# A graph attention and convolution kernel: the second ffn layer as three f32r passes, one slot for the spread row, new step orders

## The reference

```python
def _gat_heads(x, adj, W, a):                      # H heads
    Wh = einsum('bnf,hfo->bhno', x, W)
    e = f1[:, :, :, None] + f2[:, :, None, :]       # f1 = Wh.a[:O], f2 = Wh.a[O:]
    e = where(adj > 0, leaky_relu(e), -1e9)
    return softmax(e) @ Wh

h   = relu(layernorm(x))
h1  = elu(_gat_heads(h, adj, W_heads, a_heads))     # 4 heads, joined to 1024 features
out = elu(_gat_heads(h1, adj, W_out, a_out))        # 1 head, 256 features
ffn = relu(out @ w1 + b1) @ w2 + b2
x   = x + layernorm(ffn + out) * gamma + beta
h   = relu(layernorm(x))
x   = x + deg * (h @ Wi.T + b) + adj @ (h @ Wj.T)
```

## Time and profile before

| | |
|---|---|
| median of 3 runs | 1364.8 us (1364.24 to 1365.14) |
| profiled execution | 1362.21 us |
| its span | 1360.4 us |
| PE busy | 1305.1 us, 96% |
| weight loads (PEld) busy | 1254.3 us, 92% |
| DVE busy | 1095.9 us, 81% |
| ACT busy | 1116.3 us, 82% |
| POOL busy | 371.1 us, 27% |
| mean granted TensorE clock | 0.991 |

### The profile page before, as it was taken

The page is one execution under the profiler, slowest core; times in us unless marked ns, Lnnn a source line. Parts: engine busy times, 40 slices in busy tenths (PEclk is TensorE's granted clock), DMA queues, the critical chain, the costliest instruction groups (busy, mean ns, idle before and its releaser), DMA issues.

```text
span 1360.4 us, 27728 instructions
## 1 busy us (share of the span) xinstructions
PE 1305.1 (96%) x10109; PEld 1254.3 (92%) x10109; DVE 1095.9 (81%) x2848; ACT 1116.3 (82%) x2152; POOL 371.1 (27%) x252
## 2 busy tenths in 40 slices
...
DMA packets 42206, 53.32 MB, mean 39 GB/s; under 512 B 2836, under 2 KB 30808, under 8 KB 42072
## 3 DMA queue, kind: packets, MB, share of 16 engines
...
...
## 4 chain that ended last, share of the span: by engine, by line
PE 79%; DVE 10%; ACT 6%; issue 4%; DMA 1%; POOL 1%; SPq 0%; ACTq 0%; DVEq 0%; POOLq 0%
PE ps L1101 59%; PE ps L1214 8%; PE ps L1316 4%; PE ps L1280 3%; DVE arg L986 2%; DVE prob_lo L957 1%; ACT arg L785 1%; PE ps L1253 1%; PE ps L1290 1%; ACT prob_hi L791 1%; DVE arg L1012 1%; DVE st L939 1%; PE ps L1176 1%; DVE elu L1023 1%; DVE whx_lo L957 1%
## 5 line engine op out<-in xcount | busy, mean ns | idle before, releaser
L658 POOL TENSOR_TENSOR hx_lo<-elu,hx_hi 128x512 fp32r<-128x512 f32 x128 | 166.6, 1304 | 661.6 <-ACT hx_hi L815 660.4
L1101 PE MATMUL ps<-prob_hi,whx_hi 128*128 128x256 f32 x1024 | 296.0, 289 | 2.8 <-DVE prob_lo L957 2.1
L1101 PE MATMUL ps<-prob_hi,whx_lo 128*128 128x256 f32 x1024 | 289.6, 283 | 0.0
L1101 PE MATMUL ps<-prob_lo,whx_hi 128*128 128x256 f32 x1024 | 289.5, 283 | 0.0
L785 ACT ACTIVATE arg<-arg,nmax 128x512 f32<-128x512 f32 x320 | 226.9, 712 | 3.9 <-DVE nmax L997 3.7
L957 DVE TENSOR_TENSOR prob_lo<-ps,prob_hi 128x1024 fp32r<-128x1024 f32 x160 | 195.1, 1220 | 32.4 <-ACT prob_hi L791 32.1
L781 ACT ACTIVATE arg<-arg,fcol 128x512 f32<-128x512 f32 x320 | 212.3, 714 | 8.5 <-DVE gmax L986 8.4
L986 DVE CUSTOM_DVE_ANT_0 arg<-f2bc,mask 128x512 f32<-128x512 f32 x308 | 207.3, 710 | 3.6 <-PE ps L1214 3.0
L1101 PEld LDWEIGHTS ps<-prob_hi,whx_hi 128*128 128x128 f32 x1024 | 195.9, 191 | 6.5 <-DVE prob_lo L957 3.8
L1101 PEld LDWEIGHTS ps<-prob_hi,whx_lo 128*128 128x128 f32 x1024 | 196.1, 191 | 0.3
L1101 PEld LDWEIGHTS ps<-prob_lo,whx_hi 128*128 128x128 f32 x1024 | 195.9, 191 | 0.0
...
## 6 DMA issues: line engine op xcount, KB each, us to landing
...
f_rows<-f2row SPq DMA_DIRECT2D x77, 2.0 KB
...
```

The lines of the kernel that those rows point to most:

```text
L658: pool.tensor_tensor(out=hx[1][:, 2 * c.h:2 * c.h + 2, c.u * HN:(c.u + 1) * HN], in0=elu[:, c.buf, :, :], in1=hx[0][:, 2 * c.h:2 * c.h + 2 ...
L1101: i = pe.matmul(out, a, b_, start=(k == 0), stop=(k == n - 1))
```

## The change

The second ffn layer uses `product` as well: `w2` is split once into `w2w` (high and low part), and `midT` is a pair of f32r tiles. To make them, ACT now writes the relu back to PSUM in place, waits for it, and copies it rounded to SBUF as the high part; DVE subtracts that from PSUM to get the low part. `midT` lies in the buffers of `outT`, which `ffn1` has finished reading by then. The PSUM pair of `ffn1` is released by the low part (`mid_lo`), not by the relu. `f2bc` has one slot in place of two. The place where w1 is staged moves to the one slot, and w2 is staged in a part of `arg`. All orders of steps (FIRST, ROUND, LAST) are new; ROUND_FROM, ROUNDS go from 8, 8 to 10, 7.

```diff
-    F2S = 2
+    F2S = 1
-        w2_sb = sb("w2_sb", [P, KC, F])
+        w2w = [sb(f"w2_{s}", [P, KC, F], f32r) for s in ("hi", "lo")]
-        w1_st = f2bc[:, 1, :].rearrange("p (k o) -> p k o", k=KC)
+        w1_st = f2bc[:, 0, :].rearrange("p (k o) -> p k o", k=KC)
+        w2_st = arg[:, 2, 1, :].rearrange("p (k o) -> p k o", k=KC)
-        midT = ff[:, 1, :, :].rearrange("p c f -> p (c f)").rearrange("p (k n) -> p k n", k=KC)
+        midT = outT
 ...
             def w1_prep(c):
                 act.wait_ge(ld[LD_W1], 16)
                 act.activation(w1x[0][:, :, :], w1_st, ACT.Copy).then_inc(s_w1_hi, 1)
+                act.wait_ge(ld[LD_W2], 16)
+                act.activation(w2w[0][:, :, :], w2_st, ACT.Copy).then_inc(s_w1_hi, 1)
 ...
                     act.wait_ge(f1_done, KC * (c.n - 1) + o + 1 if len(c.tiles) == NC else KC * c.n)
-                    act.activation(midT[:, o, c.cols], ffn1_out(c, o), ACT.Relu,
-                                   bias=b1c[:, o:o + 1]).then_inc(f1_read, 1)
+                    act.activation(ffn1_out(c, o), ffn1_out(c, o), ACT.Relu, bias=b1c[:, o:o + 1]).then_inc(f1_relu, 1)
+                for o in range(KC):
+                    act.wait_ge(f1_relu, KC * (c.n - 1) + o + 1)
+                    i = act.activation(midT[0][:, o, c.cols], ffn1_out(c, o), ACT.Copy)
+                i.then_inc(mid_hi, 1)
 ...
             def w1_low(c):
                 dve.wait_ge(s_w1_hi, 1)
                 dve.tensor_tensor(out=w1x[1][:, :, :], in0=w1_st, in1=w1x[0][:, :, :].bitcast(fp32), op=ALU.subtract).then_inc(s_w1, 1)
+                dve.wait_ge(s_w1_hi, 2)
+                dve.tensor_tensor(out=w2w[1][:, :, :], in0=w2_st, in1=w2w[0][:, :, :].bitcast(fp32), op=ALU.subtract).then_inc(s_w1, 1)
 ...
+            def ffn1(c):
+                dve.wait_ge(mid_hi, c.n)
+                for o in range(KC):
+                    i = lo(midT[1][:, o, c.cols], ffn1_out(c, o), midT[0][:, o, c.cols])
+                i.then_inc(mid_lo, 1)
 ...
-                lend((c.pair,), (f1_read, KC * c.n))
+                lend((c.pair,), (mid_lo, c.n))
 
             def ffn2(c):
                 if c.b == 0:
-                    pe.wait_ge(ld[LD_W2], 16)
-                pe.wait_ge(f1_read, KC * c.n)
+                    pe.wait_ge(s_w1, 2)
+                pe.wait_ge(mid_lo, c.n)
 ...
-                    for k in range(KC):
-                        i = pe.matmul(y, midT[:, k, n * P:(n + 1) * P], w2_sb[:, k, :], start=(k == 0), stop=(k == KC - 1))
+                    i = product(y, [(midT[0][:, k, n * P:(n + 1) * P], midT[1][:, k, n * P:(n + 1) * P], w2w[0][:, k, :], w2w[1][:, k, :])
+                                    for k in range(KC)])
```

The order of PE in the repeating period, before and after, begins differently but is the same round:

```diff
-    f2turn:2@5 turn_p:2@5 m1:00@4 turn_gc@7 turn_p:3@5 m1:01@4 attend:2@5 conv_in:0@7 f2turn:3@5 conv_in:1@7 turn_p:4@6
-    attend:3@5 m1:10@4 turn_p:5@6 attend:4@6 turn_p:6@5 f2turn:0@4 attend:5@6 m1:11@4 conv@7 turn_out@6 attend:6@5 turn_p:7@5
-    turn_p:8@5 ffn1@6 f2turn:1@4 attend:7@5 attend:8@5 turn_p:9@5 m1:20@4 m1:21@4 ffn2@6 m1:30@4 attend:9@5 mix2:0@5
-    turn_p:0@4 mix2:1@5 turn_p:1@4 mix2:2@5 mix2:3@5 attend:0@4 f2turn:-1@5 m1:31@4 turn_in@3 attend:1@4
+    f2turn:1@5 attend:7@6 attend:8@6 turn_p:9@6 ffn2@7 m1:20@5 m1:21@5 attend:9@6 mix2:0@6 m1:30@5 mix2:1@6 turn_p:0@5
+    mix2:2@6 turn_p:1@5 mix2:3@6 attend:0@5 m1:31@5 f2turn:-1@6 turn_in@4 attend:1@5 f2turn:2@5 turn_p:2@5 m1:00@4 turn_gc@7
+    turn_p:3@5 m1:01@4 attend:2@5 conv_in:0@7 turn_p:4@6 f2turn:3@5 conv_in:1@7 attend:3@5 turn_p:5@6 m1:10@4 attend:4@6
+    turn_p:6@5 attend:5@6 m1:11@4 f2turn:0@4 conv@7 turn_out@6 attend:6@5 turn_p:7@5 turn_p:8@5 ffn1@6
```

```diff
+    f2turn:0@5 args:8@6 turn_out@7 elu_neg:6@6 elu_exp:6@6 probs:7@6 args:9@6 probs:8@6 ffn1@7 f2turn:1@5 elu_neg:7@6
...
+    probs:2@7 m1:00@6 rowmax:4@8 turn_gc@9 rowmath:4@8 rowmax:5@8 probs:3@7 m1:01@6 rinv:4@8 scale:4@8 rowmath:5@8 elu_out:2@7
+    conv_in:0@9 rowmax:6@7 rinv:5@8 rowmath:6@7 scale:5@8 probs:4@8 rowmax:7@7 conv_in:1@9 rinv:6@7 scale:6@7 elu_out:3@7
+    probs:5@8 norm_in@5 m1:10@6 elu_out:4@8 rowmath:7@7 probs:6@7 rowmax:8@7 rinv:7@7 rowmath:8@7 elu_out:5@8 scale:7@7
+    m1:11@6 rowmax:9@7 rinv:8@7 scale:8@7 conv@9 rowmath:9@7 turn_out@8 norm_in_out@5 elu_out:6@7 probs:7@7 rinv:9@7 probs:8@7
+    scale:9@7 rowmax:0@6 ffn1@8 elu_out:7@7 elu_out:8@7 rowmath:0@6 probs:9@7 rowmax:1@6 m1:20@6 ffn2@8 norm_ff@8 rinv:0@6
...
+    norm_in_out:1@0 mask:1@0 turn_in@0 w1_low@0 gc_turn@0 turn_in:1@0 m1:00@0 mask_end:1@0 norm_in@1 wo_prep:0@0 wo_prep:1@0
+    m1:01@0 wo_prep:2@0 wo_prep:3@0 rowmax:0@0 rowmath:0@0 m1:10@0 norm_in_out@1 rowmax:1@0 wo_prep:4@0 m1:11@0 rinv:0@0
...
+    turn_p:7@-1 turn_p:8@-1 ffn1@-2 attend:7@-1 attend:8@-1 turn_p:9@-1 ffn2@-2 attend:9@-1 mix2:0@-1 mix2:1@-1 mix2:2@-1
+    mix2:3@-1 f2turn:-1@-1 f2pe:-1@-1 turn_gc@-2 conv_in:0@-2 turn_p:4@-1 conv_in:1@-2 turn_p:5@-1 attend:4@-1 attend:5@-1
+    conv@-2 turn_out@-1 turn_out:1@-1 ffn1@-1 ffn1:1@-1 ffn2@-1 ffn2:1@-1 turn_gc@-1 turn_gc:1@-1 conv_in:0@-1 conv_in:1@-1
...
+    norm_ff@-2 hx_lo:9@-1 gamma@-2 norm_gc@-2 bias@-2 add_b2@-1 norm_ff@-1 x_beta@-1 norm_ff:1@-1 gamma@-1 gamma:1@-1
```

More of the change, by code:

```diff
@@ L19 @@
[L19 to L23, removed]
@@ L57 @@
+    m1:11@3 conv@0 rowmath:9@2 rinv:8@2 turn_out@1 scale:8@2 elu_out:6@2 probs:7@2 probs:8@2 rinv:9@2 rowmax:0@3 ffn1@1
+    elu_out:7@2 scale:9@2 rowmath:0@3 elu_out:8@2 probs:9@2 rowmax:1@3 ffn2@1 norm_ff@1 m1:20@3 rinv:0@3 rowmath:1@3 scale:0@3
+    elu_out:9@2 rowmax:2@3
     """,
     "POOL": """
-    norm_in@0 norm_in:1@0 norm_in@1 hx_lo:0@0 hx_lo:1@0 hx_lo:2@0 hx_lo:3@0 x_beta@0 hx_lo:6@0 hx_lo:7@0 hx_lo:8@0 hx_lo:9@0
-    norm_in@2 hx_lo:0@1 hx_lo:1@1 hx_lo:2@1 hx_lo:3@1 norm_in@3 hx_lo:6@1 hx_lo:7@1 add_b2@0 hx_lo:8@1 norm_ff@0 hx_lo:9@1
@@ L84 @@
+    elu_exp:7@6 hx:6@6
     """,
     "DVE": """
[L86 to L89 removed]
@@ L234 @@
-    scale:4@-1 conv@-2 rinv:5@-1 scale:5@-1 probs:4@-1 probs:5@-1 elu_out:4@-1 turn_out@-1 elu_out:5@-1 turn_out:1@-1 ffn2@-1
-    norm_ff@-1 norm_ff_out@-1 ffn2:1@-1 norm_ff:1@-1 x2@-1 norm_ff_out:1@-1 norm_gc@-1 x2:1@-1 norm_gc_out@-1 norm_gc:1@-1
-    norm_gc_out:1@-1 turn_gc@-1 turn_gc:1@-1 conv_in:0@-1 conv_in:1@-1 conv@-1 conv:1@-1
+    rinv:1@-6 m1:21@-6 m1:30@-6 norm_ff_out@-8 scale:1@-6 rowmath:2@-6 mix2:0@-7 rowmax:3@-6 rowmath:3@-6 probs:0@-6 x2@-8
+    probs:1@-6 rinv:2@-6 mix2:1@-7 norm_gc@-8 elu_out:0@-6 scale:2@-6 m1:31@-6 norm_gc_out@-8 rinv:3@-6 turn_in@-5 scale:3@-6
@@ new lines @@
+    conv@-6 rowmath:9@-4 scale:7@-4 scale:8@-4 turn_out@-5 elu_out:6@-4 probs:7@-4 probs:8@-4 rowmax:0@-3 rinv:9@-4 scale:9@-4
+    ffn1@-5 elu_out:7@-4 rowmax:1@-3 probs:9@-4 rowmath:0@-3 elu_out:8@-4 m1:20@-3 norm_in_out@-2 ffn2@-5 norm_ff@-5
+    rowmax:2@-3 norm_ff_out@-5 rinv:0@-3 rowmath:1@-3 rowmath:2@-3 elu_out:9@-4 scale:0@-3 m1:21@-3 rinv:1@-3 rowmax:3@-3
+    scale:1@-3 rowmath:3@-3 mix2:0@-4 probs:0@-3 m1:30@-3 x2@-5 norm_gc@-5 mix2:1@-4 rinv:2@-3 probs:1@-3 elu_out:0@-3
+    norm_gc_out@-5 m1:31@-3 rinv:3@-3 scale:2@-3 turn_in@-2 scale:3@-3 elu_out:1@-3 probs:2@-3 m1:00@-2 rowmax:4@-4
```

403 lines of the change are left out of this document (207 added, 196 removed).

## The result

The changed kernel takes 1370.6 us (median of 7 runs, 1368.0 to 1372.9), the kernel before, measured beside it, 1364.2 us (7 runs). The ratio is 1.0051, with a 95% interval of 1.0041 to 1.0061: slower by half a per cent, where 9.1 us less were forecast. Its profiled execution took 1371.99 us, with a span of 1370.2.

The account below looks back on a forecast made before the run. PE's own stream was taken as the bound in the middle, DVE in the first 70 us. Terms -8.9 (PE), +1.0 (start), -1.2 (tail) sum to -9.1: 1353.1 us profiled, 1355.7 us median, range 1349 to 1362.

Parts of the forecast that it names:

- PE's stream: ffn2 on PE: 24 f32r matmuls replace the float32 block, 2.87 for 3.46 us; 0.59 us less a batch, 8.9 over 15.
- The rival with 0.108 us a pass: ffn2's passes run at the float32 pace: 0.87 us saved a batch, 13.1 in all, 1351.5 us; chance 0.05.
- ACT and DVE: Added copies and subtractions, +1.2 and +1.3 us a period: 69.6 and 68.4 of some 78.8 us busy, no new bound.
- The wait at turn_p:9: PE waiting for mid_lo after ffn1: none taken, range 0 to 0.5 us a period; as rival 1360 us, chance 0.13.
- The slot: One slot for f2's broadcast: 5.5 us of DVE work covers issue and landing (3.6, 4.7 at worst), so zero cost.
- The rival's shape: Single slot makes broadcasts late at each of 77 hand-overs; at 0.2 us each 1371 us; chance 0.06.
- The start: DVE bounds the first 70 us and runs 2 to 4 us later; loss of 1 us taken; dearer-start rival 5 us, chance 0.10.
- The tail: Work behind the last mix2: 3.1 us less, then 1.9 more for x_beta between the norms; net 1.2 less.

Follow-up runs that it names:

- e2_orders: The changed kernel's orders and one slot for the spread f2, with the float32 second layer of the kernel before: 1378.1 us, ratio 1.0106.
- e4_slot: The kernel before with one slot for the spread f2 in place of two, nothing else changed: 1385.9 us, ratio 1.0165.
- The splices: Changed kernel, each engine following the old order up to a seam, then the new: seam at 22 us 1374.8 us, at 123 us 1360.8, at 259 us 1357.5.
- s1: Changed kernel with norm_in of batch 1 and wo_prep:0 to 3 moved later in VectorE's order of the start: 1371.0 us, ratio 1.0062.
- s2: Changed kernel with the whole adjacency chain (loads, cast, turn, wo_prep) and norm_in of batch 1 put later in the start: 1375.5 us, ratio 1.0086.
- h6_start_259: Changed kernel with the old order on all engines up to steps started there before 259 us, w2 staged in xb: 1357.5 us, ratio 0.9957.

## Why the prediction was wrong, step by step

- **PE's stream: right, a little large.** 0.59 us a batch were forecast. The block takes 2.94 us and saves 0.52, the period 0.50, since the first matmul of the step needs 0.21 to the next and not 0.12. It does so behind the float32 transposes of `turn_p:9`; where another product stands ahead of it (976.12), the first needs 0.12 and the block takes 2.85. 15 times 0.50 are 7.5, and after against e2_orders measured 7.5. That the two agree to the digit is luck: the new orders with the float32 layer have a period of 79.34, so the passes alone save 0.44, and from a0 to the end the two profiles differ by 5.0. The rival with 0.108 us a pass is out: between 729.92 and 732.53 are 22 steps of 0.1186.
- **ACT and DVE: right, DVE 1.2 too high.** 69.53 and 67.25 busy in the period, 69.6 and 68.4 forecast.
- **The wait at turn_p:9: none, as taken.** PE is busy 78.90 of 78.90. The closeness of the working (0.1 us) was a warning all the same: in the old orders the passes with this chain cost 15.5 us.
- **The slot: nothing, as taken, and for the reason given.** The cover that was counted in the new round is there. What the step did not see is that this was no property of the slot: in the old closing order it costs 22 us. The rival's shape, 0.2 us at each of 77 hand-overs, does not occur: the rounds of e4_slot have one such wait a period, and nearly all of the cost comes in seven waits of the closing order.
- **The start: this step failed.** +1.0 was taken, from a range of -2 to +5; it was +13.5. The step took DVE for the bound of the first 70 us, counted its work in list order ("2 to 4 us later than before at the same amount of work"), which leaves out idle time and the clock, and gave PE credit for filling its waits. But DVE was idle 16.7 of the first 30 us, 14.0 before, and 3.2 of the next 30, 0.7 before; its bound was read from one window of 40 to 50 us. PE's wait for `m1:01` (5.11 us, its longest for another engine in the start) stood in the order list, behind `norm_in` and two `wo_prep`. And behind its waits PE ran at the lower clock: 0.72 granted from 30 to 60 us, 0.89 before. The splices show that the order of the start makes the loss, most of it between 22 and 123 us. Since single moves gained nothing (s1, s2), which set of steps does it stays open, and so does how much of it is the clock.
- **Missing altogether: the passages between tables.** a3 to a5 takes 160.8 in place of 158.8, where two periods of the new round would be 157.8 (PE waits 0.9 and 1.3 us where FIRST ends), and the passage to the closing orders costs 5.1 us, 6.7 with a dip of the clock. The prediction priced one period and two ends. It said that PE's 55.3 idle us lie at the ends, but the four numbers that it named are 48.4; the other 6.9 lay in the middle, where these passages are (the old periods behind a9 are 79.7, 80.2 and 82.1).
- **The tail: wrong twice, with opposite signs.** From the end of the last `mix2:3` to the end it took 65.7 us, before 60.0: +5.7, where -1.2 was summed. To the last addition of the second half's ffn it was 36.8, before 35.5, or 36.4 with the 0.9 of turn_gc that the sum adds; a fall of 3.1 was summed. And behind it, with x_beta between the two norms, 28.9 in place of 24.5. But from a12 to that `mix2:3` the new closing order needs 305.5 in place of 317.1, which the prediction didn't look at: from 1200 to 1280 us PE is busy for 78.31 in place of 75.13. Net 5.9 us gained.

So one term of the sum was off by 12.5 us, the passages stood in no term, and the tail's two errors together gave a gain that hid part of them. The forecast gain would nearly have come with the old start (h6_start_259, 6.5 us), but partly by luck, since it has the unforeseen passages and the unforeseen closing order too.
